# Gated cross-attention with a quantised feed-forward on one core: the last quarter of the second weight's ternary values one step later on VectorE

## The chip, the core and the metric

One core of a Trainium2 chip. The metric is the device time of one execution of the whole kernel, in microseconds. Three runs of the kernel before gave 216.01, 216.11 and 216.25 us; their median is 216.11 us.

## The reference

For 16 sequences of 128 tokens with 256 channels, a cross-attention with 16 heads is added to the input through a gate, and then a feed-forward block with ternary weights, a convolution along the sequence and a second quantised projection. Cut to what matters:

```python
x = x + tanh(g_xattn[0]) * attention(layernorm(x), ctx, ctx, Wq, Wk, Wv, Wo)
x = x + tanh(g_ffn[0]) * ffn(layernorm(x))

def act_quant(x):                       # per token
    scale = 127.0 / clip(max(abs(x), axis=-1), 1e-05)
    return clip(round(x * scale), -128, 127) / scale

def weight_quant(w):                    # per weight: values -1, 0, 1 times one number
    scale = 1.0 / clip(mean(abs(w)), 1e-05)
    return clip(round(w * scale), -1, 1) / scale

def ffn(x):
    h = act_quant(x) @ weight_quant(w1).T         # 256 -> 1024
    h = silu(depthwise_conv1d(h, conv_w, conv_b)) # three taps along the sequence
    return act_quant(h) @ weight_quant(w2).T      # 1024 -> 256
```

## The kernel before

**The work by steps.** The 16 sequences go through a software pipeline whose order is written out by hand, once for each engine; the engines are kept together by semaphores alone, and each runs its own list in order. `step(s)` exists for TensorE, ScalarE and VectorE, and the GpSimd list has a loop over s. In step s sequence s has its scores made (`row_stage`), sequence s-1 is weighed and normalised, sequence s-2 gets its output projection and first residual, and sequence s+1 its keys, values and queries. From step 6 on each step also makes two hidden tiles of the feed-forward (`hidden`): `TILES` gives tiles 0 and 1 to step 6, 2 and 3 to step 7, and so on. A tile is 128 hidden channels of four sequences; its three convolution taps are spread over ScalarE (`middle_tap`, L1033, and the product `outer_product`, L1046), VectorE (`first_tap`, L1295) and GpSimd (`add_tap`, L484), one step after the tile was made. The even tile of a step is scaled on GpSimd (L465, from `raw`, a copy that ScalarE makes, L1019), the odd one on VectorE (L1286, from PSUM).

**VectorE in a step** (L1325 to L1346): the maxima of sequence s for its first pair of head groups (`row_max(b, 0)`, L1238), the first residual with its statistics (`residual1`, L1262 to L1268), the first tap of the last step's even tile, the shift of the queries (`shift_q`, L1246, two instructions into `Qs`), `extra(0)`, the first tap of the last step's odd tile, `normalise` (L1255, L1257, into `att`), the maxima of sequence s+1 for the other pair (`row_max(n, 1)`), `quantise1` (L1272 to L1278, into `qa`), the scaling of the odd tile, and `extra(1)`. `extra` is where a step carries work that belongs to no sequence.

**TensorE in a step**: the output projection (L695, the first of a step, so that its start marks the step here), values (L601), `weigh` (L673), the transpose of the maxima (L624), queries (L616), the transpose of `U` (L683), the even hidden tile (L753), the first half of the scores with the next maxima (L650, L660), the odd hidden tile (L753), the transpose of `att` (L689), keys (L592), and the second half of the scores. That second half waits for `row_max(n, 1)`, and the transpose of `att` for `normalise`.

**GpSimd in a step** (its loop calls `norm2`, `add_tap` of the even tile, `dequantise`, `round1`, `norm1`, `add_tap` of the odd tile): the second layer norm's scale and shift (L434, L437, L439), which waits for the statistics of `residual1`; L484; L465; the rounding (L449, L457), which waits for `qa`; the normalised queries' input of sequence s+2 (L428, L430); L484. ScalarE applies the shift of L439 in `norm2_copy` (L984, into `xn2`), and only then makes `raw` (L1019).

**The ternary values** of the two weights are made on VectorE in quarters by `ternary` (L1310 to L1318), each quarter in three `tensor_scalar` instructions over 128 x 512 values, SBUF to SBUF: scale and clip above (L1314), clip below and round (L1316), subtract the rounding constant (L1318, into `w1q` or `w2q`). `pieces` (L1394) hands two quarters to a step, one to `extra(0)` and one to `extra(1)`:

```python
step(3, pieces(0, w1f, w1q, 0, wq1_step, w1q_done))
step(4, pieces(2, w1f, w1q, 0, wq1_step, w1q_done, scale=1))
step(5, pieces(0, w2f, w2q, 1, wq2_step, w2q_done))
dve.wait_ge(small_in, 16)
step(6, pieces(2, w2f, w2q, 1, wq2_step, w2q_done))
for s in range(SB + 3, NB - 1):
    step(s)
```

`w2q` is first read in step 14, where `w2_column_sums` waits for all four quarters.

Of the kernel before, what the change touches and what calls it, by code (L numbers as in the profile page):

```python
# [14 lines left out]
NB = 16  # L15
# [12 lines left out]
SB = 4  # L28
# [40 lines left out]
def seq(i):  # L69
    return 0 <= i < NB  # L70


def build(nc, x, xTd, ctxT, wqT, wkT, wvT, woT, w1T, w2T, cwb, gates, out):
    norm_dram = nc.dram_tensor("norm_dram", (2 * NB, P), F32, kind="Internal").ap()
    with ExitStack() as stack:
        def sb(name, shape, dt=F32):
            return stack.enter_context(nc.sbuf_tensor(name, shape, dt))
# [4 lines left out]
        def sem(name):  # L82
            return stack.enter_context(nc.semaphore(name))
# [12 lines left out]
        w2f = sb("w2f", [P, NC_ * D])  # L96
        w1q = sb("w1q", [P, KD * HID], BF16)
        w2q = sb("w2q", [P, NC_ * D], F16)
# [93 lines left out]
        wq1_step, wq2_step, w1q_done, w2q_done = sem("wq1_step"), sem("wq2_step"), sem("w1q_done"), sem("w2q_done")  # L192
# [1025 lines left out]
        def _(dve):  # L1218
# [14 lines left out]
            def row_max(n, pair):  # L1233

                dve.wait_ge(max_ready, PG * (NP * n + 2 - pair))

                dst = smax[:, :].rearrange("p (t g e d) -> p g t e d", t=KD, g=NG, e=2)[:, pair * PG:(pair + 1) * PG, :, :, 0]
                dve.tensor_reduce(dst, first_max(n, pair)[:, :].rearrange("p (g t e k) -> p g t e k", g=PG, t=KD, e=2),  # L1238
                                  AX.X, ALU.max).then_inc(max_done, 1)

            def shift_q(b):
                dve.wait_ge(mT_ready, b + 1)
                dve.wait_ge(q_done, b + 1)

                for e in range(2):
                    tt = dve.scalar_tensor_tensor(  # L1246
                        Qs[:, :].rearrange("p (t e q) -> p t e q", t=KD, e=2)[:, :, e, :],
                        ps_maxT.rearrange("p (t q) -> p t q", t=KD), max_row[:, e:e + 1],
                        QT[b % 2][:, :].rearrange("p (t q) -> p t q", t=KD), ALU.mult, ALU.add)
                tt.then_inc(shift_done, 1)  # L1250

            def normalise(a):
                av = ps_uT[:, :].rearrange("p (h w) -> p h w", w=ROW)
                dve.wait_ge(uT_ready, a + 1)
                dve.reciprocal(rden[:, :].unsqueeze(2), av[:, :, DH:DH + 1]).then_inc(rden_done, 1)  # L1255
                dve.wait_ge(rden_done, a + 1)
                dve.tensor_tensor(att[:, :].rearrange("p (h w) -> p h w", w=DH), av[:, :, 0:DH],  # L1257
                                  rden[:, :].unsqueeze(2).broadcast_to([P, NH, DH]), ALU.mult).then_inc(att_done, 1)

            def residual1(a):  # L1260
                dve.wait_ge(o_ready, a + 1)
                dve.scalar_tensor_tensor(at(a), ps_o, gate[:, 0:1], at(a), ALU.mult, ALU.add).then_inc(x1_done, 1)  # L1262
                dve.wait_ge(x1_done, a + 1)
                wait(dve, mv2_done, a)
                dve.bn_stats(stats2[:, :], at(a)).then_inc(st2_done, 1)
                dve.wait_ge(st2_done, a + 1)
                wait(dve, xn2_done, a)
                dve.bn_aggr(mv2[:, :], stats2[:, :]).then_inc(mv2_done, 1)  # L1268

            def quantise1(d):  # L1270
                dve.wait_ge(xn2_done, d + 1)
                dve.tensor_reduce(qa[:, 0:1], xn2[:, :], AX.X, ALU.max,  # L1272
                                  apply_absolute_value=True).then_inc(amax_done, 1)
                dve.wait_ge(amax_done, d + 1)
                wait(dve, xq_ready, d)
                dve.tensor_scalar(qa[:, 1:2], qa[:, 0:1], EPS_Q, 1.0 / QMAX, ALU.max, ALU.mult).then_inc(qstep_done, 1)
                dve.wait_ge(qstep_done, d + 1)
                dve.reciprocal(qa[:, 2:3], qa[:, 1:2]).then_inc(qrec_done, 1)  # L1278

            def dequantise(T):  # L1280
                G = T // NC_
                dve.wait_ge(h_ready, T + 1)
                dve.wait_ge(xq_done, 2 * SB * (G + 1))
                if T >= HB:
                    finished(dve, T - HB)
                dve.tensor_tensor(hid[T % HB][:, :], ps_h[:, :], deq[:, G * GT:(G + 1) * GT],  # L1286
                                  ALU.mult).then_inc(scaled_dve, 1)
# [17 lines left out]
            def outer_taps(T):  # L1305
                first_tap(T)
                if not tap_on_gp(T):
                    last_tap(T)

            def ternary(k, wf, wt, i, step_done, done):  # L1310
                n = KD * HID // PIECES
                wf, wt = wf[:, k * n:(k + 1) * n], wt[:, k * n:(k + 1) * n]
                dve.wait_ge(scale_done, i + 1)
                dve.tensor_scalar(wf, wf, w_scale[:, i:i + 1], 1.0, ALU.mult, ALU.min).then_inc(step_done, 1)  # L1314
                dve.wait_ge(step_done, 2 * k + 1)
                dve.tensor_scalar(wf, wf, -1.0, ROUND, ALU.max, ALU.add).then_inc(step_done, 1)  # L1316
                dve.wait_ge(step_done, 2 * k + 2)
                dve.tensor_scalar(wt, wf, ROUND, None, ALU.subtract).then_inc(done, 1)  # L1318
# [6 lines left out]
            def step(s, extra=lambda k: None):  # L1325
                b, n, a, d = s, s + 1, s - 1, s - 2
                tiles, last = TILES.get(s, ()), TILES.get(s - 1, ())
                if seq(b):
                    row_max(b, 0)
                if seq(d):  # L1330
                    residual1(d)
                for T in last[0:1]:
                    outer_taps(T)
                shift_q(b)
                extra(0)
                for T in last[1:2]:
                    outer_taps(T)
                if seq(a):
                    normalise(a)
                if seq(n):  # L1340
                    row_max(n, 1)
                if seq(d):
                    quantise1(d)
                for T in tiles[1:2]:
                    dequantise(T)
                extra(1)  # L1346
# [38 lines left out]
            def weight_scale(i):  # L1385
                dve.wait_ge(sums_ready, i + 1)
                dve.tensor_scalar(w_mean[:, i:i + 1], ps_setup[:, 2 + i:3 + i], 1.0 / (HID * D), EPS_Q,
                                  ALU.mult, ALU.max).then_inc(mean_done, 1)
                dve.wait_ge(mean_done, i + 1)
                dve.reciprocal(w_scale[:, i:i + 1], w_mean[:, i:i + 1]).then_inc(scale_done, 1)  # L1390
                if i == 1:
                    dve.tensor_scalar(w_deq[:, 0:1], w_mean[:, 1:2], gate[:, 1:2], None, ALU.mult).then_inc(deq_done, 1)

            def pieces(first, *weight, scale=None):  # L1394
                def part(k):
                    ternary(first + k, *weight)
                    if scale is not None and k == 1:
                        weight_scale(scale)
                return part
# [10 lines left out]
            step(4, pieces(2, w1f, w1q, 0, wq1_step, w1q_done, scale=1))  # L1410
            step(5, pieces(0, w2f, w2q, 1, wq2_step, w2q_done))
            dve.wait_ge(small_in, 16)
            step(6, pieces(2, w2f, w2q, 1, wq2_step, w2q_done))
            for s in range(SB + 3, NB - 1):
                step(s)
            last_step()

# [110 lines left out]
```

## Time and profile before

| | |
|---|---|
| median of three runs | 216.11 us |
| the profiled execution: its own time | 215.48 us |
| its span, first to last instruction | 213.7 us |
| TensorE busy (matmul) | 197.2 us, 92% of the span |
| VectorE busy | 180.5 us, 84% |
| ScalarE busy | 158.1 us, 74% |
| GpSimd busy | 145.8 us, 68% |
| mean granted TensorE clock | 0.992 of full speed |

The profiled execution took 215.48 us, 1.78 us more than its span and 0.63 us less than the median. Steps 6 to 14 lie between about 64 and 147 us from the start of the span; what follows is the last sequence's attention and the rest of the feed-forward. In the rows PE is TensorE, DVE VectorE, ACT ScalarE and POOL GpSimd. Busy times of engines overlap, so they don't add up to the span. An instruction's duration in the trace runs from its dispatch to its end: when it is held up after dispatch, the duration grows.

### The profile page before, as it was taken

The page shows a single profiled execution, that of the slowest core. Times are in us where ns is not written, and L with a number is a line of the kernel's source. Part 1 is how long each engine was busy: PE and PEld are TensorE (multiplying, and loading weights), DVE is VectorE, ACT ScalarE, POOL GpSimd, SP SyncE. Part 2 cuts the span into 40 slices and gives each one's busy share as a digit, 9 for nine tenths or more (in the row PEclk, how much of TensorE's full clock was granted, in tenths as well). Part 3 has the DMA queues.
Part 4 walks back from the last instruction along what each step waited for, and adds up shares of the span by engine and source line. Part 5 has one row for each costly group of instructions (what it writes and reads, how often), then busy time and mean ns, then how long its engine had stood idle before and what let it go on. Part 6 is the DMA issues. An engine that isn't in the chain of part 4 may idle for free.

```text
span 213.7 us, 6119 instructions
## 1 busy us (share of the span) xinstructions
PE 197.2 (92%) x2258; PEld 161.2 (75%) x2258; DVE 180.5 (84%) x384; ACT 158.1 (74%) x272; POOL 145.8 (68%) x215
## 2 busy tenths in 40 slices
PE   6899899999999998999999999999989849898895
PEld 6788779778788877887887888777757736776784
DVE  4366769998999997998988989888899989998982
ACT  2347576675867879998998999898989855975541
POOL 2620320853427569878989888897878898999871
PEclk9999999999999999999999999999999997999999
DMA  5999411113022120202302010000002224486743
GB/s 148 306 342 285 152 29 53 39 51 87 17 74 47 45 87 15 74 17 74 66 25 64 14 28 14 5 15 0 3 0 49 52 49 104 94 101 172 127 127 121
DMA packets 29120, 16.95 MB, mean 79 GB/s; under 512 B 17546, under 2 KB 28834, under 8 KB 29090
## 3 DMA queue, kind: packets, MB, share of 16 engines
q1 hardware_dynamic: 29090, 16.55, 30.1%
q8 instruction: 18, 0.29, 0.6%
q14 instruction: 12, 0.10, 0.2%
HBM read 10.50 MB, written 2.11 MB: 59 GB/s over the span
## 4 chain that ended last, share of the span: by engine, by line
POOL 41%; issue 21%; PE 20%; DVE 11%; DMA 3%; ACT 2%; POOLq 0%; SPq 0%; DVEq 0%; ACTq 0%
POOL y L484 11%; POOL hid L465 4%; POOL w2f L472 4%; POOL xT L428 4%; POOL xT L430 3%; POOL xn L449 3%; POOL rstd L437 3%; PE ps_score L650 2%; POOL var L434 2%; POOL xq L457 2%; PE ps_av L673 2%; DVE smax L1238 2%; PE ps_proj L616 2%; PE ps_max L660 2%; PE ps_proj L880 2%
## 5 line engine op out<-in xcount | busy, mean ns | idle before, releaser
L1238 DVE TENSOR_REDUCE smax<-ps_max 128x8 f32<-128x1024 f32 x31 | 37.9, 1222 | 11.1 <-PE ps_max L660 8.4
L995 ACT ACTIVATE prob<-ps_score 128x1024 f32<-128x1024 f32 x32 | 32.6, 1020 | 9.7 <-PE ps_score L650 9.1
L484 POOL TENSOR_TENSOR y<-y,tap 128x508 f32<-128x508 f32 x30 | 39.0, 1303 | 0.9 <-DVE y L1295 0.6
L650 PE MATMUL ps_score<-Qs,KT 32*128 32x128 f32 x512 | 37.1, 282 | 0.8 <-DVE smax L1238 0.3
L650 PEld LDWEIGHTS ps_score<-Qs,KT 32*128 32x128 f32 x512 | 31.2, 186 | 8.2 <-issue 4.1
L660 PE MATMUL ps_max<-KT,QT 32*128 32x256 f32 x248 | 35.1, 400 | 0.0
L1295 DVE SCALAR_TENSOR_TENSOR y<-hid,conv,y 128x508 f32<-128x508 f32 x24 | 24.1, 1009 | 0.8 <-ACT y L1033 0.8
L449 POOL TENSOR_SCALAR xn<-xn,qa 128x256 f32<-128x256 f32 x16 | 8.5, 533 | 22.6 <-DVE qa L1278 22.5
L660 PEld LDWEIGHTS ps_max<-KT,QT 32*128 32x128 f32 x248 | 21.1, 184 | 0.1
L472 POOL TENSOR_SCALAR w2f<-y,zmax 128x1024 f16<-128x1024 f32 x16 | 17.9, 1119 | 2.6 <-DVE zmax L1426 1.4
L1421 DVE TENSOR_REDUCE zmax<-y 128x1 f32<-128x1024 f32 x16 | 19.3, 1208 | 0.1
L1033 ACT ACTIVATE y<-hid,conv 128x512 f32<-128x512 f32 x24 | 18.6, 807 | 0.2 <-POOL hid L465 0.2
L695 PE MATMUL ps_proj<-wo,attT 128*128 128x256 f32 x64 | 17.9, 402 | 0.0
L1246 DVE SCALAR_TENSOR_TENSOR Qs<-ps_score,max_row,QT 128x256 f32<-128x256 f32 x32 | 13.9, 476 | 4.4 <-PE ps_score L624 4.4
L970 ACT ACTIVATE KT<-ps_proj,shift_row,head_mask 128x256 f32<-128x256 f32 x32 | 16.3, 563 | 1.4 <-PE ps_proj L592 1.2
L673 PE MATMUL ps_av<-prob,V 128*32 128x128 f32 x512 | 17.3, 276 | 0.1
L673 PEld LDWEIGHTS ps_av<-prob,V 128*32 128x32 f32 x512 | 13.0, 109 | 5.6 <-issue 4.7
L592 PE MATMUL ps_proj<-cin,wk 128*128 128x128 f32 x128 | 17.0, 276 | 0.0
L601 PE MATMUL ps_proj<-wv,cin 128*128 128x256 f32 x64 | 16.5, 381 | 0.0
L753 PE MATMUL ps_h<-xqT,w1q 128*128 128x512 bf16 x48 | 14.4, 381 | 2.0 <-DVE hid L1286 0.9
L592 PEld LDWEIGHTS ps_proj<-cin,wk 128*128 128x128 f32 x128 | 15.5, 192 | 0.1
L1046 ACT ACTIVATE tap<-hid,conv 128x508 f32<-128x508 f32 x22 | 15.5, 712 | 0.0
(143 smaller groups left out, 488.7 us busy)
## 6 DMA issues: line engine op xcount, KB each, us to landing
cin<-ctxT SPq DMA_DIRECT2D x16, 128.0 KB, 3.3
xres<-x SPq DMA_DIRECT2D x16, 128.0 KB, 4.8
out<-xres SPq DMA_DIRECT2D x16, 128.0 KB, 1.7
xT<-xT SPq DMA_DIRECT2D x12, 128.0 KB, 2.2
norm_bc<-norm_dram SPq DMA_DIRECT2D x12, 128.0 KB, 3.3
w1f<-w1T SPq DMA_DIRECT2D x1, 1024.0 KB, 7.7
w2f<-w2T SPq DMA_DIRECT2D x1, 1024.0 KB, 7.1
wk<-wkT SPq DMA_DIRECT2D x1, 256.0 KB, 2.7
```

Of the source, the lines that this page charges most:

```text
L472: gp.tensor_scalar(zq[v % ZQ][:, :], z[v], zmax[:, 4 * v + 2:4 * v + 3], ROUND16, ALU.mult, ALU.add).then_inc(zq_done, 1)
L484: gp.tensor_tensor(y3[:, :, 0:P - 1], y3[:, :, 0:P - 1], tap_buffer(T), ALU.add).then_inc(conv_gp, 1)
L592: mm = pe.matmul(ps_k[:, t * P:(t + 1) * P], wk[:, k * D + t * P:k * D + (t + 1) * P], cin[n % CB][:, k * P:(k + 1) * P], start=(k == 0), ...
L650: mm = pe.matmul(ps_score[:, i * 512 + j * P:i * 512 + (j + 1) * P], KT[b % 3][rows, j * P:(j + 1) * P], Qs[rows, j * P:(j + 1) * P], star ...
L660: mm = pe.matmul(into[:, i * 512 + t * 2 * P:i * 512 + (t + 1) * 2 * P], QT[n % 2][rows, t * P:(t + 1) * P], KT[n % 3][rows, t * 2 * P:(t ...
L673: mm = pe.matmul(ps_av[g * ROW:(g + 1) * ROW, j * P:(j + 1) * P], V[a % VB][:, h * ROW:(h + 1) * ROW], prob[g // PG][:, (g % PG * GH + j) ...
L695: mm = pe.matmul(ps_o, attT[:, t * P:(t + 1) * P], wo[:, t * D:(t + 1) * D], start=(t == 0), stop=(t == KD - 1))
L995: act.activation(prob[pair][:, :], ps_score[:, :], ACT.Exp, scale=DH ** -0.5).then_inc(exp_done, 1)
L1033: act.activation(y_tile(T), by_sequence(hid[T % HB][:, :]), ACT.Identity, bias=conv[:, 4 * c + 3:4 * c + 4], scale=conv[:, 4 * c + 1:4 * c ...
L1238: dve.tensor_reduce(dst, first_max(n, pair)[:, :].rearrange("p (g t e k) -> p g t e k", g=PG, t=KD, e=2), AX.X, ALU.max).then_inc(max_done, 1)
L1295: dve.scalar_tensor_tensor(y3[:, :, 1:P], h3[:, :, 0:P - 1], conv[:, 4 * c:4 * c + 1], y3[:, :, 1:P], ALU.mult, ALU.add).then_inc(tap0_don ...
L1421: dve.tensor_reduce(m[:, 0:1], z[v], AX.X, ALU.max, apply_absolute_value=True).then_inc(zmax_step, 1)
```

## The change

The list `pieces(2, w2f, ...)` is no longer given to step 6 whole. Step 6 keeps its first part, the third quarter of the second weight, in `extra(0)`. The last quarter, which stood in `extra(1)` at the end of step 6, is made in `extra(0)` of step 7, directly behind `shift_q` and ahead of the first tap of tile 1. Nothing is added or left out, and all other engines' lists stay as they are.

```diff
             step(5, pieces(0, w2f, w2q, 1, wq2_step, w2q_done))
             dve.wait_ge(small_in, 16)
-            step(6, pieces(2, w2f, w2q, 1, wq2_step, w2q_done))
-            for s in range(SB + 3, NB - 1):
+            second_half = pieces(2, w2f, w2q, 1, wq2_step, w2q_done)
+            step(6, lambda k: second_half(0) if k == 0 else None)
+            step(7, lambda k: second_half(1) if k == 0 else None)
+            for s in range(8, NB - 1):
                 step(s)
             last_step()
```

VectorE at the seam of steps 6 and 7, the difference of the two orders (L1286 ends step 6's own work, the first L1238 opens step 7, the row L1246 is the shift of the queries):

```order
+L1238 TENSOR_REDUCE smax<-ps_max 128x2x2x2
+L1262 SCALAR_TENSOR_TENSOR xres<-ps_proj,gate,xres 128x256
+L1265 BN_STATS stats<-xres 128x6
+L1268 BN_AGGR mv<-stats 128x2
+L1295 SCALAR_TENSOR_TENSOR y<-hid,conv,y 128x4x127
+L1246 SCALAR_TENSOR_TENSOR Qs<-ps_score,max_row,QT 128x2x128 x2
 L1314 TENSOR_SCALAR w2f<-w2f,w_scale 128x512
 L1316 TENSOR_SCALAR w2f<-w2f 128x512
 L1318 TENSOR_SCALAR w2q<-w2f 128x512
-L1238 TENSOR_REDUCE smax<-ps_max 128x2x2x2
-L1262 SCALAR_TENSOR_TENSOR xres<-ps_proj,gate,xres 128x256
-L1265 BN_STATS stats<-xres 128x6
-L1268 BN_AGGR mv<-stats 128x2
-L1295 SCALAR_TENSOR_TENSOR y<-hid,conv,y 128x4x127
-L1246 SCALAR_TENSOR_TENSOR Qs<-ps_score,max_row,QT 128x2x128 x2
 L1295 SCALAR_TENSOR_TENSOR y<-hid,conv,y 128x4x127
```

The three ternary instructions stood ahead of the six rows that open step 7; now these come first, and the ternary ones stand between the shift of the queries and the first tap of tile 1.

GpSimd in step 7, the same in both orders (L434 to L439 are the second layer norm's numbers, L484 the tap of tile 0, L465 the scaling of tile 2, L449 the rounding), with what each instruction waits for:

```order
L434 TENSOR_SCALAR var<-mv 128x1 [waits mv2_done]
L437 TENSOR_TENSOR rstd<-var,minus_half 128x1 [waits xn2_done,var2_done]
L439 TENSOR_SCALAR shift<-mv,rstd 128x1 [waits rstd2_done]
L484 TENSOR_TENSOR y<-y,tap 128x4x127 [waits tap2_done,tap0_done]
L465 TENSOR_TENSOR hid<-raw,deq 128x512 [waits xq_done,raw_done]
L449 TENSOR_SCALAR xn<-xn,qa 128x256 [waits xq_ready,qrec_done]
```

Nothing moved here. `mv2_done` comes from the statistics that VectorE makes at the start of step 7, so this list starts when those are done, and `qrec_done` from `quantise1`, which on VectorE comes behind `normalise` and the maxima.

## Rows read from the trace of the kernel before

**Rows 1.** Windows, TensorE's steps 7 to 10: range, busy time per engine, clock, DMA
```profile
core 0: us, PE busy (x) PEld busy (x) DVE busy (x) ACT busy (x) POOL busy (x), PEclk, DMA share, GB/s
73.56:83.61 10.05, 9.30 (x122) 7.36 (x118) 8.93 (x18) 8.33 (x16) 7.93 (x11) 1.00 0.16 48
83.61:92.61 9.00, 9.00 (x121) 7.28 (x118) 8.34 (x15) 8.43 (x16) 6.67 (x9) 1.00 0.21 54
92.61:101.85 9.24, 9.07 (x122) 7.33 (x118) 8.26 (x16) 8.34 (x16) 8.10 (x11) 1.00 0.19 51
101.85:110.85 9.00, 9.00 (x121) 7.33 (x117) 7.86 (x15) 8.33 (x16) 7.67 (x11) 1.00 0.25 54
```

**Rows 2.** Timeline, TensorE, steps 7 and 8: start, duration, instruction, idle before
```profile
80.87 0.60 PE L753 MATMUL ps_h<-xqT,w1q 128*128 128x512 bf16 x2 [0.74 <-ACT raw L1019]
81.31 0.38 PE L689 MATMUL ps_proj<-ident,att 128*128 128x128 f32 x2
...
82.52 0.38 PE L650 MATMUL ps_score<-Qs,KT 32*128 32x128 f32 x2
...
83.61 1.13 PE L695 MATMUL ps_proj<-wo,attT 128*128 128x256 f32 x4
...
89.87 0.61 PE L753 MATMUL ps_h<-xqT,w1q 128*128 128x512 bf16 x2
```

**Rows 3.** Timeline, ScalarE, step 7
```profile
79.73 0.60 ACT L984 ACTIVATE xn<-xres,shift,rstd 128x256 f32<-128x256 f32 x1 [1.22 <-POOL shift L439]
80.24 0.58 ACT L1019 ACTIVATE raw<-ps_h 128x512 f32<-128x512 f32 x1
```

**Rows 4.** Timeline, GpSimd, steps 6 and 7
```profile
74.11 0.89 POOL L428 TENSOR_TENSOR xT<-xT,norm_bc 128x256 f32<-128x256 f32 x1
...
77.59 0.62 POOL L434 TENSOR_SCALAR var<-mv 128x1 f32<-128x1 f32 x1 [1.71 <-DVE mv L1268]
...
82.23 0.48 POOL L449 TENSOR_SCALAR xn<-xn,qa 128x256 f32<-128x256 f32 x1
```

**Rows 5.** Timeline, VectorE, steps 6 and 7
```profile
69.73 0.43 DVE L1318 TENSOR_SCALAR w2q<-w2f 128x512 f16<-128x512 f32 x1
...
74.46 0.83 DVE L1318 TENSOR_SCALAR w2q<-w2f 128x512 f16<-128x512 f32 x1
75.21 1.21 DVE L1238 TENSOR_REDUCE smax<-ps_max 128x8 f32<-128x1024 f32 x1
...
78.83 0.74 DVE L1295 SCALAR_TENSOR_TENSOR y<-hid,conv,y 128x508 f32<-128x508 f32 x1
...
79.77 0.42 DVE L1257 TENSOR_TENSOR att<-ps_av,rden 128x256 f32<-128x256 f32 x1
80.18 1.23 DVE L1238 TENSOR_REDUCE smax<-ps_max 128x8 f32<-128x1024 f32 x1
```

**Rows 6.** Timeline, VectorE, step 8
```profile
83.73 1.23 DVE L1238 TENSOR_REDUCE smax<-ps_max 128x8 f32<-128x1024 f32 x1 [1.00 <-PE ps_max L660]
...
87.02 0.88 DVE L1246 SCALAR_TENSOR_TENSOR Qs<-ps_score,max_row,QT 128x256 f32<-128x256 f32 x2 [0.35 <-PE ps_score L624]
87.81 1.72 DVE L1295 SCALAR_TENSOR_TENSOR y<-hid,conv,y 128x508 f32<-128x508 f32 x1
```

**Rows 7.** Timeline, GpSimd, step 8
```profile
87.72 1.27 POOL L484 TENSOR_TENSOR y<-y,tap 128x508 f32<-128x508 f32 x1
89.56 1.27 POOL L465 TENSOR_TENSOR hid<-raw,deq 128x512 f32<-128x512 f32 x1 [0.57 <-ACT raw L1019]
```

**Rows 8.** Timeline, GpSimd, in step 5 and in step 15
```profile
64.09 0.63 POOL L449 TENSOR_SCALAR xn<-xn,qa 128x256 f32<-128x256 f32 x1 [2.90 <-DVE qa L1278]
...
152.51 1.72 POOL L465 TENSOR_TENSOR hid<-raw,deq 128x512 f32<-128x512 f32 x1
```

**Rows 9.** Timeline, VectorE, beside the rows of group 8, and in step 9
```profile
64.41 0.59 DVE L1316 TENSOR_SCALAR w2f<-w2f 128x512 f32<-128x512 f32 x1
...
94.95 1.42 DVE L1295 SCALAR_TENSOR_TENSOR y<-hid,conv,y 128x508 f32<-128x508 f32 x1
...
151.84 1.26 DVE L1295 SCALAR_TENSOR_TENSOR y<-hid,conv,y 128x508 f32<-128x508 f32 x1 [0.80 <-ACT y L1033]
```

## The prediction

> **What bounds the kernel now.** I read the windows by step first. From one output projection to the next TensorE takes 9.00 us in steps 8 and 10, all of them busy, 9.24 in step 9, and 10.05 in step 7, where it is busy for 9.30 only [rows 1]. So TensorE sets the pace at 9.00 us a step, and step 7 is 1.05 us too long. That is where the change works, and the most that it can give there.
>
> The timeline of TensorE tells where most of the 1.05 lies: it stood for 0.74 us ahead of the odd hidden tile, until ScalarE's `raw` was done [rows 2]. (Step 8 reaches the same place 6.26 us after its projection, 89.87 - 83.61; step 7 took 80.87 - 73.56 = 7.31.) Backwards from there: `raw` started at 80.24, right behind `xn` (L984), which had waited 1.22 us for GpSimd's shift [rows 3]; GpSimd had waited 1.71 us for the statistics of VectorE [rows 4]; and these stand behind the maxima, which VectorE began at 75.21 as soon as the last ternary instruction was through [rows 5]. In step 8 the maxima start 0.12 us after the projection [rows 6]; in step 7 it was 1.65 us. So the last quarter's place at the end of step 6 made the maxima 1.53 us late, and TensorE paid 1.05 for that.
>
> **What goes.** With the ternary work out of the way, step 7 opens as step 8 does, 10.05 us earlier: maxima at 73.68, `Qs` at 76.97 to 77.85, `raw` in time for TensorE's odd tile at 79.82. I take step 8 of the trace as the twin of the new step 7; the same instructions stand on every engine, and the only one missing (the tap of the odd tile that GpSimd does ahead of L434 in step 8) had ended before GpSimd began to wait for the statistics. Left alone, that gains the 1.05 us.
>
> **What comes.** Three instructions now stand between `Qs` and the first tap, and behind them `normalise`, for whose `att` TensorE waits with L689, and the maxima of sequence 8, for which it waits with L650. Alone they take about 1.32 us: 0.48, 0.43 and 0.43, dispatched one right after the other (the last of the third quarter took 0.43 [rows 5]). They are not alone, though:
>
> In step 8 GpSimd dispatched its tap L484 at 87.72, 0.09 us ahead of VectorE's first tap at 87.81. L484 took its usual 1.27 and ended at 88.99; VectorE's tap took 1.72 and ended at 89.53, 0.54 behind it, where it takes 0.74 without company [rows 5 to 7]. It was held up until L484 was through. In step 15 it went both ways: VectorE's tap ended at 153.10 after a hold, and L465, dispatched at 152.51, took 1.72 instead of 1.27 and ended 1.13 after it [rows 8, 9]. Ternary instructions are held in the same manner: L1318 took 0.83 against 0.43 beside L428, which ended at 75.00; L1318 ended 0.29 later [rows 4, 5]. And a GpSimd instruction that is already waiting comes in between two ternary ones: L449 was dispatched at 64.09 and ended at 64.72; L1316, dispatched at 64.41, ended 0.28 behind it [rows 8, 9].
>
> Set into the twin (times of step 8 less 10.05):
> - L484 is dispatched at 77.67 and ends at 78.94. L1314, dispatched at 77.76, is held and ends 0.29 later, at 79.23.
> - L1316 runs from 79.25 to 79.68. L465 is dispatched at 79.51 (89.56 in the twin), gets its turn at 79.68, ends 1.13 later at 80.81.
> - L1318 is held meanwhile and ends at 81.10. The first tap, dispatched 0.08 before that end, is through at 81.76.
> - `att` is done 0.62 after the tap's end, as now (79.57 to 80.19 [rows 5]): 82.38. TensorE's L689 follows 0.06 us later at 82.44, where it started at 81.31 before.
> - From L689 to L650 TensorE takes 1.21 us [rows 2]: 83.65 against 82.52. The maxima of sequence 8 start at 82.37 and end at 83.60, just in time.
>
> So step 7 is not shorter but **1.13 us longer** than now: the 1.05 is gained ahead of the odd tile and 2.18 are lost ahead of L689: 1.32 us of work and 1.95 of holding (0.99 of L1314, 0.96 of L1318), less the 0.98 by which the twin's own tap was held and 0.1 that `att` had to spare.
>
> **Downstream.** GpSimd's rounding L449 came 2.05 us after the maxima of sequence 8 began (82.23 against 80.18), 1.38 us before the next projection at 83.61. Now it comes at 84.42, and the projection at 84.74: only 0.32 before. GpSimd enters step 8 about a microsecond nearer to TensorE, as it does step 9 in the trace, where VectorE's tap is held for 1.42 us and the step takes 9.24 [rows 1, 9]. I expect step 8 to take about 9.24 instead of 9.00, and the long and short steps to change places after that. Over the steps to 14 that is worth between nothing and 0.3; I take 0.2. What comes behind step 15 has no work that could run ahead, and should move as a whole. The last quarter's `w2q` is ready at 81 us and needed in step 14, so its lateness costs nothing; no DMA queue is passed or moved, and GpSimd's list is as before.
>
> **Sum**: -1.05 + 2.18 + 0.2 = +1.33 us. The profiled execution would go from 215.48 to 216.8; the median stood 0.63 above it, so the median goes from 216.11 to 217.4.
>
> **The unknown price** is how long the ternary instructions are held by L484 and L465, which they never meet now. From below it is nothing (no hold): 1.32 us of work, `att` at 80.43, L689 at 80.49, 0.82 earlier than now. The nearest row of the same instruction is L1318's extra 0.40 beside L428; twice that gives a step 7 as long as now. From above it is the full length, 0.99 and 0.96, which I take, because the tap in the twin shows a hold for the rest of the other's time at the very dispatch times that I expect, and L1318's 0.83 fits the same rule when its start (74.46) is set against L428's end (75.00).
>
> The Trainium skill (SBUF — State Buffer, "Who interferes with whom") says that a VectorE `tensor_scalar` from SBUF to SBUF may run in a mode that uses two ports, one pair of which it shares with GpSimd, and that whoever issues first keeps the pair for its whole instruction. By that rule both holds are at full length and the sum is the +1.33 above; by the 0.40 us of the row beside L428 alone it would be about +0.2. The trace's 1.72 us tap stands with the rule; no row shows a ternary instruction beside L484 or L465.
>
> **Rivals.**
> 1. *Ternary work goes through unhindered* (faster). It would have to be dispatched clear of both GpSimd instructions, or not be held by them. For it: in step 6 the quarter behind `Qs` ended with an unhindered 0.43 [rows 5]. Against: GpSimd had no tap to add there, the first tiles being made in that step; in step 7 it has one, and its tile behind it. Step 7 would be 0.82 shorter, with 0.2 lost downstream: 215.5. It decides if `att` is done before 81.2. Chance 0.10.
> 2. *One hold only, or two short ones.* If L465 comes after L1318 was let in, or holds it briefly, `att` is done around 81.4, L689 starts some 0.2 later than now, and with the 0.2 the median is 216.5; with two holds of 0.40 it is 216.3. Chance 0.15.
> 3. *GpSimd stays late for good.* If the late rounding makes each of four or more of the steps 8 to 14 a 9.24 us one without a short one in turn, another 0.7 to 1.0 comes on top: 218.3. Against: steps 8 to 10 fell back to 9.00 after 10.05 and 9.24. Chance 0.07.
> 4. *Step 7's loss is given back.* Later steps or the tail would have to wait less; TensorE is full in 9.00 us steps, so only the 0.24 of a long step and the waits of the tail could yield: 216.7. Chance 0.07.
>
> The forecast itself has 0.61.
>
> **How the numbers follow.** 0.2% of 216.11 is 0.43 us, about what a measurement of this kernel can tell from no change. Faster than 215.68 is rival 1: 0.10. Between 215.68 and 216.54 lie most of rival 2 and a little of rival 4: 0.14. The rest, 0.76, is slower. The range reaches from the upper half of rival 2, 216.3, to where rival 3 begins, 218.1; it leaves out rival 1, part of rival 2 and part of rival 3.
>
> **What would show it.** In the timeline of the changed kernel: the maxima of step 7 start near 73.7; ScalarE's wait of 1.22 for the shift and TensorE's 0.74 for `raw` are gone; L1314 takes about 1.45 us and L1318 about 1.4, L1316 0.43; TensorE stands for about 2 us ahead of L689 of step 7; the next L695 is near 84.7. I am wrong if the ternary instructions keep their 0.43 to 0.48, or if the projection of step 8 starts before 83.6 and the end moves with it.

## The result, and the profile after

| | before | changed |
|---|---|---|
| median, first comparison | 216.06 us (4 runs) | 217.57 us (4 runs, 217.40 to 217.72) |
| the profiled execution | 215.48 us, span 213.7 | 217.72 us, span 215.9 |

The ratio is 1.0068, with a 95% interval of 1.0056 to 1.0080: the change costs 1.5 us in this comparison. The forecast was 217.4 us, in a range of 216.3 to 218.1. Two later comparisons of the same two kernels gave 218.55 against 215.84 us and 217.81 against 216.05 us, a cost of 2.7 and 1.8 us; 218.55 lies above the range. Why the changed kernel has two times is told with the eighth experiment.

The windows of the changed kernel over TensorE's steps 7 to 10, to be set beside [rows 1]:

```profile
73.79:85.01 11.22, 9.17 (x121) 7.25 (x118) 10.49 (x18) 8.55 (x16) 6.25 (x9) 1.00 0.15 42
85.01:94.29 9.28, 9.01 (x120) 7.32 (x117) 8.24 (x16) 8.33 (x16) 8.17 (x12) 1.00 0.20 52
94.29:103.30 9.01, 8.96 (x121) 7.33 (x118) 7.86 (x15) 8.35 (x16) 7.68 (x11) 1.00 0.19 53
103.30:112.61 9.31, 8.96 (x121) 7.30 (x118) 8.10 (x16) 8.34 (x16) 7.87 (x11) 1.00 0.18 52
```

Step 7 went from 10.05 to 11.22 us and step 8 from 9.00 to 9.28. VectorE counts as busy for 10.49 us of step 7, and 1.93 us of that is time for which two of its instructions were held (below). This execution came to step 7 at 73.79 instead of 73.56, so its times are 0.23 later than those of before from the start. VectorE's timeline in step 7, for [rows 5]:

```profile
73.92 1.23 DVE L1238 TENSOR_REDUCE smax<-ps_max 128x8 f32<-128x1024 f32 x1 [0.20 <-PE ps_max L660]
...
77.99 1.46 DVE L1314 TENSOR_SCALAR w2f<-w2f,w_scale 128x512 f32<-128x512 f32 x1
79.48 0.43 DVE L1316 TENSOR_SCALAR w2f<-w2f 128x512 f32<-128x512 f32 x1
79.94 1.38 DVE L1318 TENSOR_SCALAR w2q<-w2f 128x512 f16<-128x512 f32 x1
81.24 0.73 DVE L1295 SCALAR_TENSOR_TENSOR y<-hid,conv,y 128x508 f32<-128x508 f32 x1
...
82.18 0.42 DVE L1257 TENSOR_TENSOR att<-ps_av,rden 128x256 f32<-128x256 f32 x1
82.52 1.22 DVE L1238 TENSOR_REDUCE smax<-ps_max 128x8 f32<-128x1024 f32 x1
```

GpSimd's timeline beside it, for [rows 4]:

```profile
76.31 0.62 POOL L434 TENSOR_SCALAR var<-mv 128x1 f32<-128x1 f32 x1 [0.62 <-DVE mv L1268]
...
77.91 1.26 POOL L484 TENSOR_TENSOR y<-y,tap 128x508 f32<-128x508 f32 x1
79.75 1.29 POOL L465 TENSOR_TENSOR hid<-raw,deq 128x512 f32<-128x512 f32 x1 [0.58 <-ACT raw L1019]
84.55 0.48 POOL L449 TENSOR_SCALAR xn<-xn,qa 128x256 f32<-128x256 f32 x1 [3.51 <-DVE qa L1278]
```

The maxima start 0.13 us after the projection, no longer 1.65, and GpSimd's wait for the statistics is 0.62 instead of 1.71. But L484 (77.91 to 79.17) lies over L1314, which takes 1.46 us instead of 0.48 and ends 0.28 after it. L465 was dispatched at 79.75 in the middle of L1316, got its turn at 79.91 when that ended, and was through at 81.04; L1318 waited for it and ended 0.28 later. TensorE's timeline, for [rows 2]:

```profile
82.66 0.44 PE L689 MATMUL ps_proj<-ident,att 128*128 128x128 f32 x2 [2.00 <-DVE att L1257]
...
83.92 0.38 PE L650 MATMUL ps_score<-Qs,KT 32*128 32x128 f32 x2
...
85.01 1.13 PE L695 MATMUL ps_proj<-wo,attT 128*128 128x256 f32 x4
...
91.56 0.60 PE L753 MATMUL ps_h<-xqT,w1q 128*128 128x512 bf16 x2 [0.21 <-ACT raw L1019]
```

The wait of 0.74 us ahead of the odd tile of step 7 is gone, and one of 2.00 us ahead of L689 has come.

**Where the 2.2 us between the two profiled executions lie.** 0.23 ahead of step 7, 1.17 in step 7, 0.36 in steps 8 to 14, and 0.44 behind (windows of the two kernels: 83.61 to 147.18 against 85.01 to 148.94, and then to the end):

```profile
83.61:147.18 63.57, 63.22 (x824) 51.08 (x820) 56.43 (x105) 57.83 (x105) 53.85 (x69) 1.00 0.14 34
147.18:213.70 66.52, 56.35 (x482) 44.82 (x478) 57.88 (x117) 45.85 (x65) 54.60 (x70) 0.97 0.38 80
```

```profile
85.01:148.94 63.93, 62.84 (x816) 51.08 (x819) 56.16 (x106) 57.78 (x105) 55.16 (x71) 1.00 0.13 34
148.94:215.90 66.96, 56.77 (x479) 45.53 (x478) 57.21 (x117) 45.64 (x65) 55.05 (x70) 0.95 0.37 80
```

The first 0.23 precedes everything that was changed. The last part lies behind the change and varies between executions of the same kernel: the changed kernel's second profile (experiment 8) took 66.55 us for it and its third (experiment 10) 66.94. It doesn't follow the granted clock: experiment 4 took 66.52 us there at a mean of 0.95, where before took the same 66.52 at 0.97. What makes the 0.4 us is open. Step 7 and steps 8 to 14 alone make 1.53, near the 1.51 between the medians.

### The profile page after: what moved, and what is told of

Same layout as the page of the kernel before. It is cut to its first block, busy times and chain, and to the rows that moved or that the text cites. A ratio compares the mean times of both kernels' runs of the same rounds, so it can differ in the third digit from the quotient of the medians.

```text
span 215.9 us, 6107 instructions
## 1 busy us (share of the span) xinstructions
PE 198.2 (92%) x2246; PEld 163.1 (76%) x2258; DVE 181.1 (84%) x384; ACT 158.1 (73%) x272; POOL 145.9 (68%) x215
## 4 chain that ended last, share of the span: by engine, by line
POOL 37%; PE 23%; issue 22%; DVE 13%; ACT 2%; DMA 2%; POOLq 0%; DVEq 0%; ACTq 0%
POOL y L484 8%; POOL hid L465 4%; POOL w2f L472 3%; POOL xT L428 3%; POOL xT L430 3%; POOL xn L449 3%; POOL rstd L437 3%; PE ps_av L565 3%; PE ps_score L650 2%; POOL var L434 2%; DVE y L1295 2%; PE ps_proj L592 2%; PE ps_av L673 2%; POOL xq L457 2%; DVE smax L1238 2%
## 5 line engine op out<-in xcount | busy, mean ns | idle before, releaser
L1238 DVE TENSOR_REDUCE smax<-ps_max 128x8 f32<-128x1024 f32 x31 | 37.9, 1223 | 11.2 <-PE ps_max L660 8.6
L484 POOL TENSOR_TENSOR y<-y,tap 128x508 f32<-128x508 f32 x30 | 38.9, 1300 | 1.0 <-DVE y L1295 0.6
L650 PE MATMUL ps_score<-Qs,KT 32*128 32x128 f32 x512 | 37.1, 282 | 0.8 <-DVE smax L1238 0.3
L650 PEld LDWEIGHTS ps_score<-Qs,KT 32*128 32x128 f32 x512 | 31.2, 186 | 8.1 <-issue 4.5
L449 POOL TENSOR_SCALAR xn<-xn,qa 128x256 f32<-128x256 f32 x16 | 9.1, 571 | 25.7 <-DVE qa L1278 25.6
L1295 DVE SCALAR_TENSOR_TENSOR y<-hid,conv,y 128x508 f32<-128x508 f32 x24 | 23.1, 965 | 0.8 <-ACT y L1033 0.8
L592 PE MATMUL ps_proj<-cin,wk 128*128 128x128 f32 x128 | 17.7, 283 | 0.0
L1246 DVE SCALAR_TENSOR_TENSOR Qs<-ps_score,max_row,QT 128x256 f32<-128x256 f32 x32 | 13.9, 475 | 4.4 <-PE ps_score L624 4.4
L592 PEld LDWEIGHTS ps_proj<-cin,wk 128*128 128x128 f32 x128 | 16.3, 199 | 0.1
L465 POOL TENSOR_TENSOR hid<-raw,deq 128x512 f32<-128x512 f32 x10 | 13.2, 1321 | 1.8 <-ACT raw L1019 1.8
```

The source lines that it names most:

```text
L465: gp.tensor_tensor(hid[T % HB][:, :], raw[:, :], deq[:, G * GT:(G + 1) * GT], ALU.mult).then_inc(scaled_gp, 1)
L484: gp.tensor_tensor(y3[:, :, 0:P - 1], y3[:, :, 0:P - 1], tap_buffer(T), ALU.add).then_inc(conv_gp, 1)
L592: mm = pe.matmul(ps_k[:, t * P:(t + 1) * P], wk[:, k * D + t * P:k * D + (t + 1) * P], cin[n % CB][:, k * P:(k + 1) * P], start=(k == 0), ...
L650: mm = pe.matmul(ps_score[:, i * 512 + j * P:i * 512 + (j + 1) * P], KT[b % 3][rows, j * P:(j + 1) * P], Qs[rows, j * P:(j + 1) * P], star ...
L1295: dve.scalar_tensor_tensor(y3[:, :, 1:P], h3[:, :, 0:P - 1], conv[:, 4 * c:4 * c + 1], y3[:, :, 1:P], ALU.mult, ALU.add).then_inc(tap0_don ...
```

## The experiments

The theory: from step 7 on GpSimd has the tap L484 and the tile L465 to work on, and these hold up a ternary instruction that is dispatched beside them, for the rest of their time. The rivals: any work in that place costs as much (the place alone); the 1.05 us of step 7 was not due to the late maxima; something of chance. The first three kernels leave the last quarter's values out. The diffs are cut to what matters, and the comments in them are added here. All times of before in this section are of runs on the same chip as the experiment.

### 1. The last quarter left out

```diff
+                if s == 1:                       # GpSimd's list
+                    gp.memset(w2q[:, 3 * KD * HID // PIECES:], 0.0).then_inc(w2q_done, 1)
...
-            step(7, lambda k: second_half(1) if k == 0 else None)
+            step(7)
```

> The last quarter of the ternary values is left out; GpSimd fills that quarter of w2q with zeros in step 1 instead. Both theories: step 7 opens on time and nothing stands behind the shift of the queries, so step 7 takes 9.0 us instead of the 10.05 of before; with steps 8 to 14 as before the time is 1.0 to 1.1 us under before, about 215.0 us. If step 7's 1.05 us had another cause than the late maxima, it stays near 216.1.

214.76 us against 215.82, ratio 0.9950 (0.9933 to 0.9967). Its windows of steps 7 and 8, and VectorE's first tap in step 7:

```profile
73.60:82.61 9.01, 9.01 (x122) 7.31 (x118) 8.33 (x15) 8.44 (x16) 6.25 (x9) 1.00 0.19 54
82.61:91.83 9.22, 9.07 (x121) 7.33 (x117) 8.14 (x15) 8.32 (x16) 8.07 (x11) 1.00 0.17 51
```

```profile
77.81 1.71 DVE L1297 SCALAR_TENSOR_TENSOR y<-hid,conv,y 128x508 f32<-128x508 f32 x1
```

So the late maxima did cost step 7 its 1.05 us. In this kernel, where nothing stands behind the shift, the tap itself is held by L484 for 1 us, as in step 8 of before [rows 6, 7], and `att` is still in time. And step 8 takes 9.22 here: behind a step 7 of 9.0 it isn't the 9.00 of before. From the start of step 7 to the end of step 14 the profile is 0.74 us shorter than before's (72.88 against 73.62), and behind step 14 another 0.26, where nothing was changed; so the 1.06 us between the medians isn't all the gain of step 7.

### 2. Three reductions in its place

```diff
+                for i in range(3):               # behind the shift of the queries in step 7
+                    dve.tensor_reduce(probe[:, i:i + 1], w1f[:, i * D:(i + 1) * D], AX.X, ALU.max)
```

> The last quarter is left out as in the first experiment, and in its place behind the shift of the queries in step 7 stand three reductions over 128x256 values in SBUF, about 0.41 to 0.45 us each, so as much VectorE work as the three ternary instructions take unhindered (1.32 us). Theory of the hold (GpSimd holds up instructions of the ternary's kind, and reductions not): none is lengthened by L484, att is done near 80.5, step 7 is about 0.8 us shorter than before, and with 0.2 to 0.3 lost in step 8 the time is 215.4 to 215.7 us. Rival (the place alone costs it: any 1.3 us of work there makes att late): like the changed kernel, 217.5 us.

214.57 us against 215.82, ratio 0.9940 (0.9926 to 0.9954). VectorE in step 7, and the window:

```profile
77.76 1.06 DVE L1423 TENSOR_REDUCE probe<-w1f 128x1 f32<-128x256 f32 x3
78.73 0.75 DVE L1298 SCALAR_TENSOR_TENSOR y<-hid,conv,y 128x508 f32<-128x508 f32 x1
```

```profile
73.55:82.56 9.01, 9.01 (x122) 7.30 (x118) 8.35 (x18) 8.44 (x16) 6.26 (x9) 1.00 0.19 52
```

The place alone is out. L484 ran from 77.66 to 78.94 beside all three reductions, and each took 0.409 us. I had counted them at their 0.41 to 0.45 one after another; without waits between them they overlap by some 0.08 us and take 1.06 together, less than the 1.32 that they stand for. Even so the outcome is clearer than foreseen: they cost nothing against the first experiment. The tap behind them was dispatched at 78.73, late in L484's time, and took 0.75 instead of 1.71; it ended at 79.48, 0.54 behind L484 as the held tap of the first experiment did. The reductions used up just the time in which it would have stood. The Trainium skill (SBUF — State Buffer, "Who interferes with whom") says that on trn2 a reduction never contends with GpSimd, while a `tensor_scalar` may: both are so here.

### 3. One ternary instruction and two reductions

```diff
+                dve.tensor_scalar(q, q, w_scale[:, 1:2], 1.0, ALU.mult, ALU.min)   # q: the last quarter of w2f
+                for i in range(2):
+                    dve.tensor_reduce(probe[:, i:i + 1], w1f[:, i * D:(i + 1) * D], AX.X, ALU.max)
```

> As the second experiment, but the first of the three is a real ternary instruction (L1314's operation on the last quarter), followed by two reductions; the quarter's values are left out. Theory of the hold with its turn-taking: the ternary instruction is held by L484 to near 1.45 us, the reductions run at 0.41 to 0.45, and L465 now gets in ahead of the first tap, which takes about 1.3 to 1.6 us instead of 0.73; att near 82.0 and the time about 217.0 us. If a hold belonged to the ternary instructions alone, the tap would keep 0.73, att would be done near 81.4 and the time be about 216.4 us. If the place alone costs it: 217.5 us.

216.62 us against 215.82, ratio 1.0034 (1.0021 to 1.0047). VectorE in step 7:

```profile
77.89 1.46 DVE L1421 TENSOR_SCALAR w2f<-w2f,w_scale 128x512 f32<-128x512 f32 x1
79.27 0.73 DVE L1423 TENSOR_REDUCE probe<-w1f 128x1 f32<-128x256 f32 x2
79.92 1.53 DVE L1298 SCALAR_TENSOR_TENSOR y<-hid,conv,y 128x508 f32<-128x508 f32 x1
```

Both holds are there at the foreseen length, 1.46 and 1.53, and the second falls on the tap, since L465 (dispatched at 79.64) now comes ahead of it. What is paid is thus not a price of the ternary instruction but one for each GpSimd instruction that gets in front of a VectorE instruction that it can hold. Step 7 takes 10.80 us, 0.42 under the changed kernel's. The total is 0.4 us under what I wrote.

### 4. The changed kernel with GpSimd's two instructions exchanged in step 7

```diff
                 for T in TILES.get(s - 1, ())[0:1]:
-                    add_tap(T)
+                    if s != 7:
+                        add_tap(T)
                 for T in TILES.get(s, ()):
                     if on_gp(T):
                         dequantise(T)
+                if s == 7:
+                    add_tap(0)
```

> The changed kernel, but in step 7 GpSimd scales tile 2 (L465) before it adds the tap of tile 0 (L484). Theory of the hold: nothing of GpSimd's stands beside the ternary instructions, they take 0.48, 0.43 and 0.43 us, the first tap gets its turn ahead of L465, att is done near 80.5, and TensorE's L650 starts 0.8 us earlier than before; step 8 is 0.2 to 0.3 long; 215.5 to 215.8 us, faster than both kernels. Rival (the ternary instructions' place alone): 217.5 us as the changed kernel.

215.12 us against 215.82, ratio 0.9967 (0.9954 to 0.9980): faster than both kernels. VectorE and GpSimd in step 7:

```profile
77.71 0.48 DVE L1317 TENSOR_SCALAR w2f<-w2f,w_scale 128x512 f32<-128x512 f32 x1
78.22 0.43 DVE L1319 TENSOR_SCALAR w2f<-w2f 128x512 f32<-128x512 f32 x1
78.68 0.43 DVE L1321 TENSOR_SCALAR w2q<-w2f 128x512 f16<-128x512 f32 x1
79.02 0.74 DVE L1298 SCALAR_TENSOR_TENSOR y<-hid,conv,y 128x508 f32<-128x508 f32 x1
```

```profile
79.46 1.43 POOL L465 TENSOR_TENSOR hid<-raw,deq 128x512 f32<-128x512 f32 x1 [1.81 <-ACT raw L1022]
80.86 1.26 POOL L484 TENSOR_TENSOR y<-y,tap 128x508 f32<-128x508 f32 x1
```

```profile
73.50:82.80 9.30, 9.23 (x122) 7.25 (x118) 8.57 (x18) 8.46 (x16) 6.38 (x9) 1.00 0.20 52
82.80:92.08 9.28, 9.07 (x121) 7.33 (x118) 8.24 (x16) 8.32 (x16) 8.15 (x12) 1.00 0.22 52
```

The ternary instructions have their own times, L465 now is the one that waits (1.43 instead of 1.29, for the tap), and L484 runs where nothing of VectorE's can be held. This is the changed kernel's work in the changed kernel's place; only its company on GpSimd differs. Step 7 is down to 9.30, 1.92 less than the changed kernel's 11.22, and the two holds there came to 1.93 (0.98 of L1314, 0.95 of L1318). The 0.30 above 9.00 is what the work costs in this place without a hold. The total fell by 0.70 us; I had written 215.5 to 215.8 with before at 216.1, a gain of 0.3 to 0.6.

### 5. The last quarter at the end of step 7

```diff
-            step(7, lambda k: second_half(1) if k == 0 else None)
+            step(7, lambda k: second_half(1) if k == 1 else None)
```

> The last quarter at the end of step 7 (extra(1)) instead of behind the shift of the queries. If 1.3 us of work at a step's end costs about a step's slack because it makes the next maxima late, step 7 takes 9.0 us and step 8 about 10.0 to 10.3 instead of 9.0: nothing is won against before, 215.8 to 216.4 us. If the 1.05 us of step 7 were a matter of step 7 alone, it would be gone: about 215 us.

216.06 us against 215.84, ratio 1.0006 (0.9997 to 1.0015), no difference from before. Windows of steps 7 and 8:

```profile
73.64:82.64 9.00, 9.00 (x121) 7.29 (x117) 8.34 (x16) 8.43 (x16) 6.25 (x9) 1.00 0.20 54
82.64:92.76 10.12, 9.37 (x121) 7.36 (x118) 9.09 (x19) 8.34 (x16) 9.16 (x12) 1.00 0.18 46
```

The loss has moved by a step with the work: it belongs to a quarter at a step's end.

### 6. The last quarter behind `normalise`

```diff
                 if seq(a):
                     normalise(a)
+                if s == 7:
+                    extra(2)                     # the last quarter
                 if seq(n):
                     row_max(n, 1)
...
-            step(7, lambda k: second_half(1) if k == 0 else None)
+            step(7, lambda k: second_half(1) if k == 2 else None)
```

> The last quarter in step 7 behind normalise, ahead of the maxima of sequence 8. Theory of the hold: the first tap meets L484 (1.7 us), L1314 meets L465 (1.0 to 1.1 us), L1316 and L1318 keep 0.43; TensorE's L689 is on time, but the maxima end near 83.2, so L650 starts 0.7 us later than before, and with 0.2 to 0.4 lost behind it the time is 216.8 to 217.2 us, between before and the changed kernel. Without holds of the ternary instruction: L650 0.1 us later, about 216.3 us.

216.97 us against 215.84, ratio 1.0051 (1.0037 to 1.0065). VectorE's quarter and TensorE's wait:

```profile
80.10 1.05 DVE L1314 TENSOR_SCALAR w2f<-w2f,w_scale 128x512 f32<-128x512 f32 x1
81.18 0.43 DVE L1316 TENSOR_SCALAR w2f<-w2f 128x512 f32<-128x512 f32 x1
```

```profile
83.35 0.38 PE L650 MATMUL ps_score<-Qs,KT 32*128 32x128 f32 x2 [1.73 <-DVE smax L1238]
```

As foreseen by the theory of the hold: 1.05 for L1314, 0.43 for L1316 and L1318, and the wait has moved from L689 (80.34, without one) to L650.

### 7. The kernel before with the exchange of experiment 4

> Control: the kernel before, with GpSimd's L465 ahead of L484 in step 7. Nothing of VectorE's is held there in before, and raw comes late (80.8), so the swap has nothing to save and puts L484 behind L465, which makes the rounding L449 about 1.2 us later: no gain, between 216.0 and 216.8 us. If the swap were a gain by itself, it would be 0.3 us or more under before here too.

216.37 us against 215.84, ratio 1.0029 (1.0017 to 1.0041): the exchange alone loses 0.5 us. GpSimd's L484 lay between 82.09 and 83.36, L449 followed at 83.33, and step 8 took 9.52 us instead of 9.00, with a wait of 0.45 us for `raw`. It pays only together with the moved quarter.

### 8 and 10. The changed kernel again

> The changed kernel once more, beside the others. If the long holds are set by the program's order and not by chance, L1314 and L1318 take 1.3 to 1.5 us each again, step 7 takes 11.2 us, and the time is 1.3 to 1.7 us above before. If step 10's wait for the transposed xq (0.35 us in the first profile) was chance, it is gone.

> The changed kernel beside the filled one on the same chip. If the clock's fall is a matter of where the idle stretch happens to lie, its runs are split: some near 217.5, some near 218.5 (1.0 to 1.3 us apart); if it belongs to the chip, all are alike.

The eighth gave 218.55 us against 215.84, ratio 1.0117 (1.0097 to 1.0138), its four runs 217.55, 218.49, 218.61 and 218.71; the tenth 217.81 against 216.05, ratio 1.0090 (1.0068 to 1.0113), with four runs from 217.25 to 217.83 and two at 218.73 and 218.91. All of step 7's holds are the same as in the first profile (1.46, 0.43 and 1.37 us in the eighth), as expected. But the eighth's time is 2.7 us above before and not 1.3 to 1.7. Its windows differ, here the eighth's for 82 to 86 us and step 7:

```profile
82.00:86.00 4.00, 3.31 (x22) 3.09 (x26) 2.98 (x8) 1.26 (x3) 1.33 (x3) 0.57 0.00 0
73.82:86.56 12.74, 10.74 (x122) 8.67 (x118) 10.54 (x18) 8.58 (x16) 7.59 (x12) 0.87 0.13 37
```

```profile
82.69 0.69 PE L689 MATMUL ps_proj<-ident,att 128*128 128x128 f32 x2 [2.00 <-DVE att L1257]
83.17 1.91 PE L592 MATMUL ps_proj<-cin,wk 128*128 128x128 f32 x8
```

At the end of the idle stretch of 2.00 us, at 82.59, the granted clock went from 1.00 to 0.50 of full speed, that is from 2.4 to 1.2 GHz, and came back at 86.00 us; the keys took 1.91 us instead of 1.06, and step 7 12.74 instead of 11.22. The tenth's profiled execution (218.91 us) shows the same, 0.57 for 82 to 86 us and a step 7 of 12.75. The first profile had the same stretch of 2.00 us and kept its 1.00. Five of the fourteen runs of this kernel lie between 218.4 and 219.0, the others between 217.2 and 217.9; the means of the two groups, 218.69 and 217.60, are 1.1 us apart. That fits the trace: of step 7's added 1.52 us 0.34 is given back, since step 8 then takes 9.00, and steps 8 to 14 63.59 instead of 63.93.

The mean granted clock of a whole execution, known for every run, tells of the runs that have no profile. The nine shorter runs have 0.983 to 0.992, like every run of before. Three of the five longer ones have 0.976, which no run of any other kernel here has; one more stretch at half clock like this one lowers the mean by 0.008. The other two, at 0.984, are the ones profiled, where the stretch is seen in step 7. So all five had such a stretch or the sign of one; only for the two profiled is it shown where.

The first profile's wait of 0.35 us in step 10, for the DMA that transposes `xq`, did not come again in the eighth or tenth. It isn't the changed kernel's own: experiments 1, 2 and 4 have it at the same place in step 10 with 0.14, 0.11 and 0.20 us, and experiment 11, the same kernel as the fourth, has none.

### 9 and 12. The idle stretch filled

```diff
+                if s == 7:                       # TensorE's list, ahead of att_transpose
+                    keep_busy(14, ps_k)
```

> The changed kernel with 14 transposes' worth of idle matmuls (identity by identity, into a free part of PSUM) on TensorE in step 7, ahead of the transpose of att, where it stood idle for 2.0 us. If the 1.5 us that the second look at the changed kernel was longer in step 7 come from the clock falling to half after that idle stretch, the granted clock stays at 1.00 around 82 to 86 us in every run, step 7 takes 11.2 us, the holds on VectorE are unchanged (about 1.45 and 1.38 us), and the runs lie at 217.0 to 217.7 us without one near 218.5. If it came from something else, some runs are still near 218.5.

219.01 us against 216.05, ratio 1.0129 (1.0106 to 1.0152), runs from 218.03 to 219.63. The stretch is filled and more:

```profile
80.36 3.29 PE L565 MATMUL ps_proj<-ident 128*128 128x128 f32 x28
83.48 0.38 PE L689 MATMUL ps_proj<-ident,att 128*128 128x128 f32 x2
```

I had taken a matmul for one entry of the trace, where it is two; the 14 took 3.1 us and kept L689 waiting to 83.48, and step 7 took 12.13 us. The clock did stay at 1.00 between 82 and 86 us, but the kernel is no test of the total time. Its profiled execution (219.08 us) is also longer behind step 14, 67.92 us against 66.96, with two waits of TensorE for a DMA there of 0.79 and 1.01 us; the changed kernel's first profile has one, of 0.74. Whether these waits make the spread of 1.6 us between its runs isn't shown. With 7 instead of 14:

> As the filled kernel, with 7 of the idle matmuls instead of 14: the 14 took 3.1 us where 2.0 were free, and so made step 7 longer by themselves; 7 take about 1.6 us and end before att is done. Theory of the clock: it stays at 1.00 around 82 to 86 us, step 7 takes 11.2 us, and the runs lie within some 0.5 us of each other between 217.2 and 217.9 us, 1.3 to 1.7 us above before, none near 218.7. If the split of the changed kernel's runs had another cause, it is still there.

217.34 us against 215.85, ratio 1.0066 (1.0053 to 1.0079), six runs from 216.85 to 217.66.

```profile
80.21 1.73 PE L565 MATMUL ps_proj<-ident 128*128 128x128 f32 x14
82.39 0.44 PE L689 MATMUL ps_proj<-ident,att 128*128 128x128 f32 x2 [0.45 <-DVE att L1259]
```

```profile
73.50:84.73 11.23, 10.78 (x135) 8.96 (x131) 10.51 (x18) 8.54 (x16) 6.26 (x9) 1.00 0.17 45
```

Step 7 takes 11.23 at a clock of 1.00 and no run is near 218.7, though the runs lie within 0.8 us and not within 0.5. With 5 of 14 runs of the changed kernel in the slower group, six without one could be luck about once in 14 times, and the changed kernel itself wasn't run beside it. So the split goes with the fall of the clock, by the clocks above; that filling the stretch prevents the fall is likely, and not proved.

### 11. The exchange once more

> The changed kernel with GpSimd's L465 ahead of L484 in step 7, once more: no long idle stretch on TensorE, no hold of the ternary instructions, 0.5 to 1.0 us under before in every round.

215.73 us against 216.05, ratio 0.9984 (0.9975 to 0.9992). Step 7 took 9.29 us and step 8 9.28, the ternary instructions 0.48, 0.43 and 0.43. The order of things is the same, the gain smaller than I wrote: 0.3 us here, 0.7 in the fourth. By the steps it should be 0.75 in step 7 less 0.28 in step 8, about 0.5; from the start of step 7 to the end of step 14 the two profiles of this kernel are 0.34 and 0.44 us shorter than before's. That it is faster than before is shown twice, the size only as 0.3 to 0.7.

## Why the prediction was right

**What bounds the kernel, and what the old place cost.** Right. The chain from the late maxima to TensorE's 0.74 us was read backwards through four engines, and the first experiment gave the whole 1.05 back in step 7; the fifth shows it move with the work.

**The twin.** Right to a few hundredths: with the 0.23 of the start taken off, L1314 came at 77.76 (77.76 foreseen), L465 at 79.52 (79.51), `att` was done at 82.37 (82.38), L689 started at 82.43 (82.44), and the projection of step 8 at 84.78 (84.74).

**The hold, the unknown price.** Right at its upper end: L1314 took 1.46 and L1318 1.38 us. The alternative, 0.40 us a piece as in the row beside L428, is not what happened; that row was a hold as well, only of an instruction dispatched late in the other's time. Experiments 2 and 3 separate the kind of instruction from the place, and 4 takes the company away. Rivals 1 and 2 are out. Rival 1 asked that the ternary instructions be clear of both GpSimd instructions. Experiment 4 makes that so, and finds rival 1's price: step 7 0.75 shorter than before (0.82 foreseen) and a total 0.70 less (0.6 foreseen).

**Downstream.** The mechanism was right, its size a little low. GpSimd's rounding came 0.46 us ahead of the projection of step 8 (0.32 foreseen, 1.38 in before), step 8 took 9.28 us (9.24 foreseen), and steps 8 to 14 took 0.36 more than before (0.2 foreseen). The other runs bear the lead out:

| kernel | rounding ahead of the projection of step 8 | TensorE's wait for `raw` in step 8 | step 8 |
|---|---|---|---|
| experiment 8, clock at half in part of step 7 | 1.98 us | none | 9.00 us |
| before | 1.38 | none | 9.00 |
| experiment 9, step 7 of 12.13 | 1.35 | none | 9.00 |
| experiment 1 | 0.52 | 0.15 | 9.22 |
| changed | 0.46 | 0.21 | 9.28 |
| experiment 6 | 0.42 | 0.24 | 9.32 |
| experiment 7 | 0.23 | 0.45 | 9.52 |

With a short lead GpSimd never waits between the rounding and the shift L439 of step 8, ScalarE waits for that shift (0.61 us in the changed kernel, 0.55 in the first experiment, not at all in before), and `raw` is late. VectorE's tap of the even tile is held by L484 on the way, as I had read it in step 9: 1.46 us in the changed kernel.

What I overlooked is that this is no consequence of the loss. In the first experiment nothing is lost in step 7, the rounding is at 82.09 and so not late, but the projection is early too. The short step 8 of before was a gift of its long step 7. "Left alone, that gains the 1.05 us" holds for step 7 alone: over steps 7 to 14 it is 0.74 in the first experiment and 0.77 in the second, whose medians are 1.06 and 1.25 below before; the rest of these is not explained by the steps.

**The sum.** Term by term, step 7 gave +1.17 (+1.13 foreseen) and steps 8 to 14 +0.36 (+0.2), 1.53 together, and the medians 1.51, against the 1.33 of the forecast. The profiled execution took 217.72 us where I had 216.8; 0.23 and 0.44 of that lie ahead of step 7 and behind step 14.

**Rival 3** (late for good) did not come: step 9 took 9.01. **Rival 4** did not either: steps 8 to 14 were longer, not shorter. **The tail** I let move as a whole; between the profiled executions it was 0.44 longer, which in the second profile of the same kernel it was not (66.55 against 66.52).

**What I didn't foresee** is the clock. I looked at TensorE's idle 2 us only as lost time; in five of fourteen runs it cost a further 1.1 us on average. That none of the four runs of the first comparison was among them is luck: with the eighth experiment's runs, three of the four in the longer group, the median would have been 218.55, above the range, with every term of the sum as it is.

## What to carry to other kernels

Work that is moved away from a full wait has to be placed by its company and not only by the free time of its own engine: look up what GpSimd does at the new time, whether the moved instructions are of a kind that it holds, and count a hold for each GpSimd instruction that comes between. A neighbouring step of the trace with the same lists is a good twin to read dispatch times from; here it was right to 0.04 us. An idle stretch that opens on TensorE can cost more than its length, as the 2.00 us here did in five of fourteen runs. When the order of two GpSimd instructions is free, exchanging them may be worth more than moving the work of VectorE, but check it with and without the move.

## What the runs showed of the hardware

- In these traces VectorE's `tensor_scalar` (SBUF to SBUF) and its taps (two SBUF inputs) take turns with GpSimd's L484 and L465 by instruction: the one that waits comes in as soon as the other's instruction has ended, even between two of a stream that follow each other within 0.03 us. A held `tensor_scalar` of 128x512 float32 ended 0.28 to 0.29 us after its holder, a held tap 0.54, a held L465 1.13.
- `tensor_reduce` from SBUF was not lengthened by L484: 0.409 us each beside it. In experiment 2 three of them filled just the time in which the held instruction would have waited, at no cost (214.57 against 214.76 us).
- At the end of an idle stretch of 2.00 us on TensorE the granted clock fell from full to half in two of three profiled executions of the same program, with the same 2.00 us in each; it stayed down from 82.59 to 86.00 us. After 1.73 us (experiment 6), 1.57 (experiment 3) and 0.45 (experiment 12) the one execution profiled of each kept full speed.
